# Reordering the recurrence slot of a decoder layer: near Gram matrices first, far factors applied on the product, small work moved to GpSimd, filler matmuls on TensorE

## The reference

```python
normed = layernorm(layernorm(x)) * ln_g + ln_b
q, k, v, beta = split(normed @ w_qkvb + b_qkvb, 4);  beta = sigmoid(beta);  k = k / norm(k)   # per head
def step(S, (q_t, k_t, v_t, beta_t)):
    retrieval = S @ k_t
    S = S + outer(beta_t * (v_t - retrieval), k_t)
    return S, S @ q_t
x = x + layernorm(x) + scan(step) @ w_out + b_out
x = x + layernorm(softmax(mask(layernorm(x) @ ctx^T / 16)) @ ctx) * gamma + beta
# feed-forward: activations quantised to int8 by the 99.5% quantile of |x|, ternary weights
x = x + qlinear(gelu(qlinear(layernorm(x), w1)), w2)
```

## Time and profile before

| | |
|---|---|
| time, median of 3 runs | 1049.23 us (1046.55 to 1050.08) |
| the profiled execution | 1049.88 us, of which the span is 1047.7 us |
| PE busy in the span | 913.1 us, 87% |
| DVE busy | 885.6 us, 85% |
| ACT busy | 655.9 us, 63% |
| POOL busy | 503.6 us, 48% |
| mean granted clock of PE | 0.936 |

### The profile page before, as it was taken

The page is one execution under the profiler, slowest core; times in us unless marked ns, Lnnn a source line. Parts: engine busy times, 40 slices in busy tenths (PEclk is TensorE's granted clock), DMA queues, the critical chain, the costliest instruction groups (busy, mean ns, idle before and its releaser), DMA issues.

```text
span 1047.7 us, 19435 instructions
## 1 busy us (share of the span) xinstructions
PE 913.1 (87%) x6084; PEld 695.0 (66%) x6091; DVE 885.6 (85%) x2603; ACT 655.9 (63%) x1597; POOL 503.6 (48%) x731
## 2 busy tenths in 40 slices
PE   7899999999999999999999998989999921895066
PEld 7577787778787877877788786766666620442044
DVE  4788899989999999999999998766677787799887
ACT  4576777656667666666666665445677750894085
POOL 5344435533554564455355545245678870970000
PEclk9799999989999999999999999999999975898589
DMA  9800000000000000001200000021420000000012
GB/s 157 141 5 8 6 7 9 9 6 7 8 10 7 6 12 6 7 9 44 92 7 11 7 6 10 20 85 59 162 76 2 1 0 1 1 1 1 1 66 96
DMA packets 28572, 30.49 MB, mean 29 GB/s; under 512 B 5548, under 2 KB 23864, under 8 KB 28472
## 3 DMA queue, kind: packets, MB, share of 16 engines
q1 hardware_dynamic: 28256, 29.12, 11.4%
q10 hardware_dynamic: 216, 0.14, 0.0%
HBM read 20.85 MB, written 4.19 MB: 24 GB/s over the span
## 4 chain that ended last, share of the span: by engine, by line
PE 76%; DVE 17%; issue 4%; ACT 2%; POOL 1%; DVEq 0%; ACTq 0%; POOLq 0%
PE ps L1911 8%; PE ps L1903 7%; PE psG L1865 6%; PE ps L1842 6%; PE psY L1879 5%; PE psX L1879 4%; PE ps L2029 4%; PE psX L1957 4%; PE psY L1957 3%; PE psG L1859 3%; PE psX L2050 2%; PE ps L1971 2%; PE ps L2217 2%; PE psY L2050 2%; PE psG L1860 2%
## 5 line engine op out<-in xcount | busy, mean ns | idle before, releaser
L550 POOL TENSOR_TENSOR arena<-arena 128x256 f32<-128x256 f32 x32 | 23.3, 729 | 304.0 <-DVE arena L1232 304.0
L687 ACT ACTIVATE arena<-ps 128x512 f32<-128x512 f32 x128 | 72.9, 596 | 40.6 <-PE ps L1903 40.3
L1903 PE MATMUL ps<-work 32*128 32x256 f32 x512 | 94.2, 409 | 2.5 <-ACT work L733 1.8
L509 POOL TENSOR_SCALAR_AFFINE_SELECT arena<-arena 128x2048 f32<-128x2048 f32 x32 | 92.1, 2877 | 2.2
L652 ACT ACTIVATE arena<-ps,nparity 32x256 f32<-32x256 f32 x124 | 51.1, 458 | 48.5 <-PE ps L1842 48.1
L1903 PEld LDWEIGHTS ps<-work 32*128 32x128 f32 x512 | 62.7, 188 | 19.8 <-issue 12.0
L1865 PE MATMUL psG<-arena 128*128 128x512 f32 x128 | 75.1, 673 | 0.5 <-DVE arena L1298 0.5
L1243 DVE TENSOR_TENSOR arena<-arena 128x256 f32<-128x256 f32 (+1 forms) x96 | 66.6, 694 | 3.5
L1842 PE MATMUL ps<-work,arena 128*128 128x64 f32 x496 | 62.1, 280 | 7.6 <-DVE work L1258 7.6
L1246 DVE TENSOR_REDUCE arena<-arena 128x64 f32<-128x256 f32 (+1 forms) x96 | 65.9, 687 | 3.3
L1879 PEld LDWEIGHTS psY<-work,arena 128*128 128x128 f32 x512 | 59.8, 195 | 12.0 <-DVE arena L1315 9.9
(11 more groups left out here) (341 smaller groups left out, 2595.9 us busy)
## 6 DMA issues: line engine op xcount, KB each, us to landing
arena<-in_mask_BxSxS_ik SPq DMA_DIRECT2D x8, 1024.0 KB, 6.6
xs<-arena SPq DMA_DIRECT2D x256, 16.0 KB, 1.8
arena<-in_ctx SPq DMA_DIRECT2D x8, 512.0 KB, 4.1
out<-xs SPq DMA_DIRECT2D x32, 128.0 KB, 1.7
arena<-in_x SPq DMA_DIRECT2D x8, 288.0 KB, 19.5
arena<-in_L_ffn_w SPq DMA_DIRECT2D x2, 1024.0 KB, 23.6
arena<-in_x SPq DMA_DIRECT2D x16, 96.0 KB, 7.1
arena<-in_L_attn_w_qkvb SPq DMA_DIRECT2D x2, 512.0 KB, 4.7
```

The lines of the kernel that those rows point to most:

```text
L509: G.affine_select(out=pairs, in_=pairs, compare_op=ALU.is_ge, fill=0.0, base=0, pattern=[[0, NH], [-CT, B], [0, CT]], channel_multiplier=1 ...
L687: A.activation(attn[j % 2][:, r * 512:(r + 1) * 512], ps[(2, 0)[r % 2]][:, :], ACT.Copy).then_inc(att_out, 1)
L1903: last = M.matmul(ps[(2, 0)[r % 2]][:, f * 2 * P:(f + 1) * 2 * P], kq[j % 4][rows, f * P:(f + 1) * P], qe[rows, f].rearrange("p e t -> p ( ...
```

## The change

What is done, part by part:

1. Order on PE. `near_gram(j+1)` moves from the slot in which it is used to the slot before, behind the queries; `far_gram(j)` moves into its own slot, ahead of attention. Between `state` and `retrieval`, where near_gram stood, now stand `turn`, `values` and `key_sums`.
2. Far factor. `scale_far` and `G1` go. `solve` reads the far Gram matrix from PSUM where it needs it (token 8) and multiplies the 128x128 sum by beta instead, one more small DVE instruction. `far_used` tells PE when psG is free.
3. Order on DVE. `scale_near(j+1)` runs ahead of the state copy, `fold_near` behind it; products and `keys_normed` follow. The one 512-wide transpose becomes two of 256, with a semaphore step each, and PE's `state` may begin after the first.
4. Key norms. The four DVE instructions become one ACT copy (`key_sums_out`) and the GpSimd chain becomes a maximum, a power and a broadcast copy.
5. `x_added` leaves DVE: ACT copies the mixed output to SBUF (`mixed_copied`), GpSimd adds it. GpSimd masks first and adds the bias after.
6. `late_inputs` leaves DVE for GpSimd, in four groups in slots 2, 4, 6 and 8.
7. `outputs` issues its 16 matmuls with the column group innermost instead of outermost.
8. ACT does its `early_work` (moments of later inputs, weight sums) ahead of emptying attention, not behind it, and loads the tables of Exp and Gelu ahead of their first use.
9. `kept_busy`, matmuls of ones into an unused bank, stands in the last three slots, in the quantile search, and ahead of both feed-forward products.

```diff
@@ solve, on DVE
                 for t in range(1, CT):
+                    if t == 8:
+                        v.wait_ge(g1_mm, 2 * (j + 1))
...
-                        src = g1 if n == 8 else g2h[:, :, a].rearrange("p h (t s) -> p h t s", s=4)
+                        src = far if n == 8 else g2h[:, :, a].rearrange("p h (t s) -> p h t s", s=4)
...
+                        if n == 8:
+                            mult.then_inc(far_used, 1)
+                            v.wait_ge(far_used, j + 1)
...
                         own(V.tensor_reduce(sums, part, AX.X, ALU.add))
+                        if n == 8:
+                            own(V.tensor_tensor(sums, sums, beta[j % 4].rearrange("p (h t) -> p h t", t=CT)[:, :, 8:16], ALU.mult))
@@ the slot on DVE
                 if exists(j) and j < NCK - 1:
                     updates_turned(j)
-                if exists(j + 1):
-                    scale_far(j + 1)
...
-                if exists(j - 1):
-                    x_added(j - 1)
                 if exists(j + 1) and j + 1 < NCK - 1:
                     keys_turned(j + 1)
                 if exists(j + 1):
+                    scale_near(j + 1)
                     state(j + 1)
-                if exists(j + 3):
-                    key_norms(j + 3)
+                    fold_near(j + 1)
+                    far_products(j + 1)
...
-                if exists(j + 1):
-                    scale_near(j + 1)
                 if exists(j + 2):
-                    far_products(j + 2)
-                if exists(j + 2):
+                    keys_normed(j + 2)
                     near_products(j + 2)
                 if exists(j + 1):
-                    if j in FACTORS_AT:
-                        late_inputs(*FACTORS_AT[j])
                     start_chunk(j + 1)
@@ GpSimd
-                ss, root, sqr = nrm
-                for n in range(3):
-                    own(G.tensor_tensor(sqr, root, root, ALU.mult))
-                    own(G.tensor_tensor(sqr, sqr, ss, ALU.mult))
-                    own(G.tensor_scalar(sqr, sqr, -0.5, 1.5, ALU.mult, ALU.add))
-                    if n < 2:
-                        own(G.tensor_tensor(root, root, sqr, ALU.mult))
+                ss, root, length = nrm
+                own(G.tensor_scalar(length, ss, NORM_EPS * NORM_EPS, None, ALU.max))
+                own(G.tensor_tensor(root, length, half, ALU.pow))
...
+            def x_added(j):
+
+                pool.wait_ge(mixed_out, j + 1)
+                pool.wait_ge(xb_ready, j + 1)
+                G.tensor_tensor(xc[:, j, :], xc[:, j, :], mixed_s, ALU.add).then_inc(x_done, 1)
@@ ACT
+            def key_sums_out(m):
+
+                act.wait_ge(n_mm, m + 1)
+                act.wait_ge(rn_ready, m)
+                A.activation(nrm[0], ps[1][:, 0:NH], ACT.Copy, scale=-1.0).then_inc(seeded, 1)
+
+            def mixed_copied(j):
+
+                act.wait_ge(w_mm, j + 1)
+                act.wait_ge(x_done, j)
+                A.activation(mixed_s, ps[2][:, 0:D], ACT.Copy).then_inc(mixed_out, 1)
@@ outputs, on PE
-                for r in range(4):
-                    for f in range(DC):
-                        for e in range(2):
+                for f in range(DC):
+                    for e in range(2):
+                        for r in range(4):
@@ PE, filler and where it stands
+            def kept_busy(into, n):
+
+                for _ in range(n):
+                    M.matmul(into[:, 0:P], ones[:, :], ones[:, :], start=True, stop=True)
...
+                elif exists(j + 1):
+                    pe.wait_ge(att_out, 4 * j + 3)
+                    kept_busy(ps[2], 4)
...
+                if j < NCK <= m:
+                    pe.wait_ge(att_out, 4 * j + 4)
+                    kept_busy(ps[0], 7)
...
+            kept_busy(ps[3], 10)
             turned(0)
...
             quantile(1)
+            kept_busy(ps[3], 24)
```

More of the change, by code:

```diff
@@ L983, in _ @@
                 if exists(j):
+                    early_work(j)
+                    early_stats(j)
+                    for _ in range(QUERIES_AT.get(j, 0)):
+                        early_query(next(early_tiles))
                     attention_out(j, 0)
@@ L991, in _ @@
                     attention_out(j, 3)
-                if exists(j):
-                    early_work(j)
-                    early_stats(j)
-                    for _ in range(QUERIES_AT.get(j, 0)):
-                        early_query(next(early_tiles))
                 if exists(j - 1):
@@ L1002, in _ @@
                     keys(m)
-                if exists(m + 1):
-                    scaled_by_feature(m + 1)
+                if m == NCK:
+                    act.wait_ge(squares_known, 3 * B)
+                    A.activation(scrap[0][:, 0:1], ones[:, 0:1], ACT.Exp)
+                if exists(j - 1):
+                    mixed_copied(j - 1)
                 if j == NCK - 1:
@@ L1061, in gelu @@
                 A.activation(gT[:, n * 512:(n + 1) * 512], ps[n % 3][:, :], ACT.Gelu, scale=deq[:, 0:1]).then_inc(gabs, 1)
+            A.activation(scrap[1][:, 0:1], ones[:, 0:1], ACT.Gelu)
             act.wait_ge(scale_ready[0], 1)
@@ L1451, in _ @@
             input_stats(1)
-            key_norms(0)
             input_sums(1)
@@ L2092, in _ @@
                         state(j - 1)
+                if j >= 1 and exists(j + 3):
+                    turn(j + 3)
+                if j >= 2 and exists(j):
+                    pe.wait_ge(oT_ready, j - 1)
+                    pe.wait_ge(c_ready, j - 1)
+                    values(j)
+                if j >= 1 and exists(j + 2):
+                    key_sums(j + 2)
                 if j >= 1 and exists(j):
-                    near_gram(j)
                     retrieval(j)
@@ L2103, in _ @@
                     pe.wait_ge(ctxT_ready, 4)
[L2104 to L2114 removed]
+                if exists(j):
+                    far_gram(j, 0)
+                    far_gram(j, 1)
+                    attention(j, 0)
+                    attention(j, 1)
                 if exists(j - 1):
                     outputs(j - 1)
+                if exists(j):
+                    attention(j, 2)
+                    attention(j, 3)
+                if exists(j + 2) and j >= 1:
+                    norms_turned(j + 2)
                 if exists(m):
```

160 lines of the change are left out of this document (76 added, 84 removed).

## The result

The changed kernel takes 1036.7 us (median of 4 runs, 1035.35 to 1039.83) against 1048.05 for the kernel before on the same chip: a ratio of 0.9891, 95% interval 0.9867 to 0.9915. It is faster by 11 us, not by the 54 predicted, and lies above the upper end of the range, 1029. The profiled execution took 1035.35 us, its span 1033.5.

A forecast was written before the change was run, and what follows sets the result against it. It took PE (19.4 us of a 20.22 us slot) as first bound, DVE (19.9) second. Savings of 42 (scan), 4 (start), 4.3 (scan's end, table) and 4.3 (products) from 1049.9 gave 995 us, range 984 to 1010, or to 1029 with two rivals.

The forecast's parts named there:

- DVE's 18.1 us a slot: DVE's work in a steady scan slot was to fall from 20.22 to 18.1 us, 0.9 below PE.
- a rival at 15%: DVE becomes the bound beside GpSimd, whose adds and broadcast fall on DVE's products: slot 19.6 us, time 1013 us; 15%.
- The outputs order: With the column group innermost, the `outputs` matmuls were to take 1.1 us in place of 2.39, saving 1.29 a slot.
- TensorE's own work in a slot: PE's steady scan slot was to go from 20.22 to 19.0 us, by savings less new waits.
- bubbles: New PE waits for ACT in each slot: 0.45 us between state and retrieval, 0.6 us ahead of queries.
- The ring: Chain of solve, transpose, state, ACT's copy and retrieval: 18.7 us a slot, only 0.3 below the bound.
- The clock falls in each slot: Rival: PE's two waits a slot lower its clock, costing 2.5 us a slot: slot 21.5 us, time 1070; 3%.
- The moments: ACT's input moments ahead of emptying attention were to delay queries 0.55 us in each of slots 0 to 7: 4.4 lost.
- Ahead of the first transpose: Before the scan's first transpose, reordered Gram matmuls and key norms leaving DVE were to save 4 us, bounds 0 and 8.
- The products and fillers: In the two feed-forward products, filler and a higher PE clock were to save 3 us and 1.3 us.
- the scan's end: In the scan's last slots filler was to keep PE's clock up and save 3 us, plus 1.3 for Exp's table.
- The late factors' stalls: DVE's stalls in irregular scan slots from late layernorm factors were to go, counted within the scan's 42 us saved.

The follow-up runs named there:

- outputs_alone: The kernel before, with the column group innermost in `outputs` and nothing else changed: 1052.9 us, ratio 1.0036.
- best: Changed kernel with DVE adding the mixed output, GpSimd's bias addition beside solve's reduction, and ACT's early work behind emptying attention: 986.7 us, ratio 0.9418.
- bias_mid: Changed kernel with the mixed output added by DVE again and GpSimd's bias addition moved into the next slot's solve: 994.7 us, ratio 0.9487.
- outputs_back: Changed kernel with the loops of `outputs` in the old order, column group outermost: 1021.1 us, ratio 0.9746.
- filler_ahead: Changed kernel with four filler matmuls of ones (1.0 us) on TensorE ahead of each state: 1030.6 us, ratio 0.9818.
- best_no_filler: Same as best, but without any filler matmul: 992.1 us, ratio 0.9448.

## Why the prediction was wrong, step by step

- **DVE's 18.1 us a slot: the step that failed.** The sum put nothing for DVE standing still beside GpSimd, and called the 0.9 us below TensorE safe. DVE takes 18.1 + 1.74 of standing still, less 0.1, the 19.72 measured, and sets the slot. I had named this as a rival at 15% with 19.6 a slot and 1013 us, and the price of its slot was about right; what was wrong was to count it as a chance. The earlier trace rows showed it, 1.44 for 1.04 us, and the row was read as a rare mishap and not as something to check for each of DVE's instructions. The check would have been simple: GpSimd's masks and additions take 6.4 us (2.0 + 2.88 + 0.73 + 0.78) from solve's end, and the new order puts only 4.0 us of transposes, PSUM reads and the copy there before the first of DVE's instructions with two SBUF operands. The Trainium skill, SBUF — State Buffer, SBUF: two separate sides, states the rule: a DVE instruction with two SBUF inputs and a GpSimd instruction that reads SBUF exclude each other for their whole length. The trace agrees for masks and additions, and for GpSimd's L523 held up by L1344; it does not for GpSimd's power of 16 columns (last section).
- **Which engine was the bound before: wrong.** The prediction has PE's own work, 19.4 us, as the first bound and DVE's, 19.9, as the second, though the second is the larger; outputs_alone shows that with PE made faster the slot stays 20.2.
- **The outputs order: right.** 1.1 us predicted, 1.01 measured. The Trainium skill, TensorE: Matmul & The Clock Gate, part 3, lets a weight load overlap only when the row group differs; here all 16 matmuls use all rows, and the order alone takes the group from 2.46 to 1.08 us. The changed kernel's 32 weight loads start and end within 0.81 us, beside the matmuls (PEld row at 440.73), so for column groups the trace says otherwise.
- **TensorE's own work in a slot: right in kind, too high.** Predicted 19.0 with 1.05 of bubbles. In best PE is busy for 18.18 of 18.67 us. The bubble ahead of retrieval is 0.33 us (0.45 predicted), that ahead of queries 0.1 (0.6 predicted).
- **The ring, 18.7: the number was right.** It is the slot of bias_mid and best, 18.67. That the ring sets it is not shown: in best DVE goes from the products into `start_chunk` without a wait, and PE is idle for 0.5 us of the slot, so ring, DVE and PE lie within half a microsecond of each other.
- **"The clock falls in each slot", 3%: came true in part.** The 28 slots from 68.2 to 636.0 us average 20.28 where the steady one is 19.72, 15.6 us in all. Four of them (21.44 three times, 22.98) follow the idle stretch of 1.1 to 1.35 us ahead of state, 8.4 us; it was made by DVE's lateness and the faster `outputs` together, and not by the two bubbles of 0.45 and 0.6 that I had it follow from. outputs_back and filler_ahead show it: no idle stretch, none of these four; outputs_alone shows the reverse. (The price of this rival took 1.8 us for the next two groups behind a fall; in the earlier trace rows state alone takes 3.68 in place of 1.90.) Two more (21.6 and 23.3, 5.5 us) follow PE's waits for ACT, which itself waited for GpSimd, and the rest, 1.7 us, is mostly five slots of 20.0 to 20.4 that outputs_back has too.
- **The moments, 4.4 us: wrong place.** The wait is all in slot 0's attention, 4.09 us with the moments ahead and 1.05 behind; with the clock, slot 1 is some 3 to 4 us longer for it.
- **Ahead of the first transpose: 9.2 saved (48.7 to 39.5), 4 predicted** with bounds of 0 and 8. Which of the edits gave the rest was not tried.
- **The last tile: left out.** Moving x_added behind ACT and GpSimd delays the last transfer. From the last transpose to the end of cross attention the changed kernel takes 200.8 us and the kernel before 198.5, where 4.3 less were predicted; the runs with the addition on DVE and the new order of `outputs` take 195.4 to 196.8.
- **The products and fillers: nearly right.** 4.3 us predicted for both products; from the end of cross attention on, the changed kernel takes 177.7 us and the kernel before 181.5, 3.8 less, of which 2.3 are the fillers by best_no_filler. Of the 3 us for the scan's end little was there to gain: the last two slots of before were 20.88 and 19.73. The filler does not gain there, it keeps the new order from losing 4.6.
- **The late factors' stalls: right, but part of them moved.** The two slots of 22.7 us around slot 8 of before are 19.7 now. At 103.78 PE waits 2.00 us for what hangs on GpSimd's factors, and slot 4 takes 21.6.

The sum for the profiled execution, from 995 to 1035: 30 steady slots at 0.72 more, +21.6; the long slots +15.6; slot 1 +1.4 beyond the 6.9 put down for moments and a cold clock; the start -5.2; behind the scan +7.1, most of it the last tile. The mended kernel's 986.7 is below the forecast of 995, but not as confirmation of it: its slot is 18.67 and not 19.0, and its start saved 4 us more than was put down.

What stays open: why of slots with the same 1.11 us of idle time some lose their clock and others not, and why slot 1, in kernels that are alike up to there, differs by 3 us with its clock.

## What to carry to other kernels

Before you move small work to an idle GpSimd, lay its instructions in time beside DVE's: here an addition of 0.7 us cost DVE 0.4 to 0.5 where it met an instruction with two SBUF operands, and nothing beside a reduction, a transpose or a read of PSUM. Ask also who waits for what GpSimd makes: the layernorm factors came late for ACT, and TensorE stood for it. And saving work on an engine that is not the bound can cost time when the idle stretch that it opens brings down that engine's clock; mend the bound first, then the same edit pays.

## What the hardware showed that was not expected

- DVE's instructions with two SBUF operands and GpSimd's masks and additions wait for each other over whole instructions: 0.29 us became 1.09 beside a mask and 1.78 in the worst place shown, and DVE's share shows as busy, never as idle. DVE's transposes and reads of PSUM ran unharmed beside masks (the copy's halves 0.68 us, alone or beside a mask), and its reduction kept 1.22 us with an addition of 0.73 wholly inside it.
- GpSimd's power of 16 columns does not hold DVE up: DVE's products beside it kept their 1.22 and 1.03 us. It is itself stretched, from 2.93 us in the changed kernel to 4.01 in best, where one of DVE's 1.22 us lies beside its start. An exclusion over the whole instruction would have cost DVE 3 us. Why the power differs from a mask or an addition, no run shows.
- The order of 16 matmuls on four column groups changes their time from 2.46 to 1.08 us.
